# Nine of ten up products in high and low f32r parts, raw weights loaded from ScalarE's queue, and new written orders for five engines

## What is computed

```python
# state space: DI = 256 channels, DS = 16 states, 256 positions, per batch b
state = state * exp(delta_t * A) + (delta_t * u_t) * B_t
y_t   = sum_n state[:, n] * C_t[n]
x = x + tanh(g_xattn) * ((y + D * u) * silu(layernorm(x)))
# experts: xf = layernorm(x); 2 shared units and 8 experts, FF = 176
h_e   = silu(xf @ wg_e.T) * (xf @ wu_e.T)
x = x + tanh(g_ffn) * (sum_shared h_e @ wd_e.T + sum_e weight_e * (h_e @ wd_e.T))
```

## Time and profile before

| | us |
|---|---|
| median of 3 runs | 282.44 |
| lowest, highest | 282.11, 283.94 |
| the profiled execution, its own time | 282.1 |
| its span, first to last instruction | 280.3 |
| busy: VectorE / TensorE / GpSimd / ScalarE | 232.8 / 228.3 / 182.8 / 178.7 |

### The profile page before, as it was taken

The page is one execution under the profiler, slowest core; times in us unless marked ns, Lnnn a source line. Parts: engine busy times, 40 slices in busy tenths (PEclk is TensorE's granted clock), DMA queues, the critical chain, the costliest instruction groups (busy, mean ns, idle before and its releaser), DMA issues.

```text
span 280.3 us, 4168 instructions
## 1 busy us (share of the span) xinstructions
PE 228.3 (81%) x1093; PEld 172.5 (62%) x1093; DVE 232.8 (83%) x590; ACT 178.7 (64%) x536; POOL 182.8 (65%) x187
## 2 busy tenths in 40 slices
PE   8823874386972869999968996899999989999994
PEld 3412652064741447878747784688778768778783
DVE  2569999999999999799999988997998899663431
ACT  3578999963785895659675896567665572251221
POOL 0029989999999999957677789857865483120000
PEclk9975797559896558999997997999999999999999
DMA  6699970000024000000007000000000000000000
GB/s 177 210 314 384 306 299 0 0 0 2 0 118 187 0 1 0 19 4 0 19 6 299 0 5 16 4 0 19 2 1 19 4 0 0 19 0 2 21 0 21
DMA packets 9560, 17.36 MB, mean 62 GB/s; under 512 B 824, under 2 KB 8800, under 8 KB 8928
## 3 DMA queue, kind: packets, MB, share of 16 engines
q1 hardware_dynamic: 9248, 16.94, 17.3%
q10 hardware_dynamic: 288, 0.16, 0.2%
HBM read 15.97 MB, written 1.11 MB: 61 GB/s over the span
## 4 chain that ended last, share of the span: by engine, by line
PE 41%; DVE 30%; POOL 14%; issue 8%; ACT 5%; DVEq 1%; POOLq 0%
PE psD L452 15%; PE psU L600 10%; DVE hs L897 6%; POOL dbu L1011 6%; DVE hs L903 5%; POOL acc L1035 5%; DVE prod L914 4%; DVE ag L985 4%; PE psM L584 4%; DVE hcat L812 3%; PE psU L610 2%; PE psU L612 2%; PE psU L611 2%; DVE xh L847 2%; PE psD L529 2%
## 5 line engine op out<-in xcount | busy, mean ns | idle before, releaser
L1011 POOL TENSOR_TENSOR dbu<-du,bb 128x512 f32<-128x512 f32 x64 | 81.9, 1293 | 31.9 <-DVE du L380 19.2
L643 ACT ACTIVATE psA<-delta,aneg 128x127 f32<-128x127 f32 (+1 forms) x256 | 79.1, 357 | 14.6 <-DVE hs L897 7.6
L1035 POOL TENSOR_TENSOR acc<-acc,prod 128x512 f32<-128x512 f32 x42 | 53.5, 1273 | 16.6 <-DVE prod L914 15.5
L600 PE MATMUL psU<-wup,hnT 128*128 128x352 f32 x160 | 59.9, 500 | 2.9 <-DVE hcat L808 1.0
L772 ACT ACTIVATE tg<-psU 128x176 f32<-128x176 f32 x80 | 24.9, 313 | 49.2 <-PE psU L600 31.4
L903 DVE TENSOR_TENSOR_SCAN hs<-psA,ends,dbu 128x128 f32<-128x128 f32 x128 | 50.9, 461 | 0.1
L452 PE MATMUL psD<-wdn,hT 128*128 128x256 f32 x224 | 50.2, 380 | 0.0
L452 PEld LDWEIGHTS psD<-wdn,hT 128*128 128x128 f32 x224 | 42.2, 190 | 6.2 <-issue 0.3
L914 DVE TENSOR_TENSOR prod<-hs,psC 128x512 f32<-128x512 f32 x64 | 43.2, 681 | 2.3 <-issue 1.4
L600 PEld LDWEIGHTS psU<-wup,hnT 128*128 128x128 f32 x160 | 30.0, 204 | 15.4 <-issue 2.9
L985 DVE SCALAR_TENSOR_TENSOR ag<-tg,psU 128x176 f32<-128x176 f32 x80 | 25.7, 327 | 15.5 <-ACT tg L772 15.4
(11 more groups left out here) (116 smaller groups left out, 327.2 us busy)
## 6 DMA issues: line engine op xcount, KB each, us to landing
bb<-brows SPq DMA_DIRECT2D x3, 2048.0 KB, 7.1
hcat<-in_w_up SPq DMA_DIRECT2D x2, 880.0 KB, 8.9
wup<-in_w_up SPq DMA_DIRECT2D x2, 880.0 KB, 11.4
wdn<-in_w_down SPq DMA_DIRECT2D x1, 1664.0 KB, 14.1
x_sb<-in_x SPq DMA_DIRECT2D x4, 256.0 KB, 6.8
bb<-brows SPq DMA_DIRECT2D x1, 1024.0 KB, 4.7
out<-outb SPq DMA_DIRECT2D x8, 128.0 KB, 1.7
sel<-in_sel SPq DMA_DIRECT2D x1, 768.0 KB, 6.0
```

The source lines that it names most:

```text
L600: last = pe.matmul(dst, hnT[:, b % 2, k, lh * P:(lh + 1) * P], wup[:, j // 2, k, :], start=(k == 0), stop=(k == KT - 1))
L643: last = act.activation(dst[:, j, h, c:], delta[:, b % 2, h, l0 + c:l1], ACT.Exp, scale=aneg[:, h * DS + s0 + j:h * DS + s0 + j + 1])
L1011: pool.tensor_tensor(tile(dbu[:, m % DBU_RING]), du[:, b % 2, :, l0:l1].unsqueeze(1).broadcast_to(shape), bb[:, b % 2, s0:s0 + NS, l0:l1]. ...
L1035: pool.tensor_tensor(acc[:, p % 2], before, prod[:, i % PROD_RING], ALU.add).then_inc(s_add, 1)
```

## The change

1. In each tile only unit j = 0 remains a plain f32 product; units 1 to 9 use f32r parts. So nine high and nine low parts of the weights are made in place of five.
2. The raw weights of units 1 to 5 and of unit 0 are loaded by DMAs issued from ScalarE's queue at the very start, ahead of all its work. Those of units 6 to 9 are loaded into the same staging memory by a new SyncE task, `weights_more:0`, once five low parts are made; it stands between `dt:0` and `xproj:1`.
3. `up:j` of the first tile waits for its own part only, and `mul:0` no longer waits for the parts.
4. All lists are written anew. The scratch memory for dynamic DMA is set to 4096 bytes.

```diff
-NSPLIT = NU // 2
+NSPLIT = NU - 1
+WSTAGE = 5
...
-        wup = sb("wup", [P, NU - NSPLIT, KT, 2 * FF])
+        wup = sb("wup", [P, KT, 2 * FF])
...
-                        for k in range(KT):
-                            sp.dma_start(staged[:, :, k], w_up[:, 1::2, k]).then_inc(d_wst, 16)
-                        for k in range(KT):
-                            sp.dma_start(wup[:, :, k], w_up[:, 0::2, k]).then_inc(d_wup, 16)
...
+                elif task == "weights_more":
+                    sp.wait_ge(s_wlo, WSTAGE)
+                    sp.dma_start(staged[:, 0:NSPLIT - WSTAGE], w_up[:, 1 + WSTAGE:NU]).then_inc(d_wst[1], 16)
...
-                            if j % 2 == 0:
+                            if j == 0:
...
-                                if unit == 1:
-                                    pe.wait_ge(s_wlo, NSPLIT)
+                                if unit < NU:
+                                    pe.wait_ge(s_wlo, j)
...
-                                    w_hi, w_lo = whi[:, j // 2, k, :], wlo[:, j // 2, k, :]
+                                    w_hi, w_lo = whi[:, j - 1, k, :], wlo[:, j - 1, k, :]
...
             act.dma_start(par[:, :], params).then_inc(d_par, 16)
+            act.dma_start(staged[:, :], w_up[:, 1:1 + WSTAGE]).then_inc(d_wst[0], 16)
+            act.dma_start(wup[:, :, :], w_up[:, 0]).then_inc(d_wup, 16)
...
-                    if i == 0:
-                        act.wait_ge(d_wst, 16 * KT)
-                    act.copy(whi[:, i], staged[:, i]).then_inc(s_whi, 1)
+                    if i % WSTAGE == 0:
+                        act.wait_ge(d_wst[i // WSTAGE], 16)
+                    act.copy(whi[:, i], staged[:, i % WSTAGE]).then_inc(s_whi, 1)
...
-                if unit == 0:
-                    dve.wait_ge(s_wlo, NSPLIT)
```

More of the change, by code:

```diff
@@ L112 @@
[L112 to L116, removed]
@@ L167 @@
-        scan:61 gate:61 prod:61 scan:62 prod:62 scan:63 mul:60 mul:61 finish:5 prod:63 gate:62 mul:62 gate:63
-        mul:63 gate_y:7 residual:7 gate:64 mul:64 stats:7 gate:65 mul:65 variance:7 gate:66 mul:66 gate:67
-        mul:67 gate:68 mul:68 gate:69 mul:69 route:7 gate:70 mul:70 gate:71 mul:71 finish:6 gate:72 mul:72
-        gate:73 mul:73 gate:74 mul:74 gate:75 mul:75 gate:76 mul:76 gate:77 mul:77 gate:78 mul:78 gate:79 mul:79
-        finish:7
+        load:0 tap0:0 tap1:0 tap2:0 silu_u:0 split0:0 z_stats:0 split1:0 split2:0 z_stats:1 log_1:0 log_2:0
@@ new lines @@
+        delta0:0 delta1:0 delta2:0 tap0:1 z_stats:2 scan:0 prod:0 scan:1 scan:2 prod:1 scan:3 tap1:1 prod:2
+        tap2:1 prod:3 scan:4 scan:5 prod:4 prod:5 z_stats:3 silu_u:1 scan:6 scan:7 prod:6 prod:7 z_gate:0 scan:8
+        scan:9 split0:1 gate_y:0 split1:1 split2:1 residual:0 prod:8 prod:9 stats:0 variance:0 scan:10 scan:11
+        prod:10 prod:11 log_1:1 scan:12 prod:12 log_2:1 scan:13 route:0 tap0:2 tap1:2 scan:14 prod:13 prod:14
+        scan:15 scan:16 gate:0 gate:1 mul:0 prod:15 prod:16 tap2:2 scan:17 prod:17 scan:18 mul:1 prod:18 gate:2
@@ new lines @@
+        silu_u:2 mul:2 gate:3 gate_y:1 mul:3 residual:1 gate:4 mul:4 scan:19 scan:20 prod:19 prod:20 stats:1
+        gate:5 gate:6 split0:2 variance:1 z_gate:1 split1:2 mul:5 split2:2 scan:21 prod:21 scan:22 mul:6 scan:23
+        prod:22 prod:23 scan:24 scan:25 gate:7 gate:8 route:1 mul:7 mul:8 prod:24 prod:25 log_1:2 scan:26
+        scan:27 gate:9 log_2:2 gate_y:2 prod:26 prod:27 mul:9 residual:2 scan:28 scan:29 stats:2 variance:2
+        prod:28 prod:29 gate:10 gate:11 mul:10 mul:11 scan:30 scan:31 prod:30 finish:0 prod:31 gate:12 mul:12
@@ new lines @@
+        gate:13 mul:13 scan:32 scan:33 gate:14 gate:15 prod:32 prod:33 route:2 mul:14 mul:15 tap0:3 tap1:3
+        gate_y:3 tap2:3 scan:34 silu_u:3 residual:3 z_gate:2 stats:3 gate:16 variance:3 prod:34 mul:16 scan:35
+        scan:36 gate:17 gate:18 mul:17 mul:18 split0:3 prod:35 prod:36 split1:3 scan:37 scan:38 split2:3 gate:19
+        prod:37 mul:19 prod:38 route:3 scan:39 scan:40 prod:39 prod:40 gate:20 log_1:3 gate:21 mul:20 mul:21
+        scan:41 scan:42 finish:1 log_2:3 prod:41 prod:42 gate:22 gate:23 mul:22 mul:23 scan:43 scan:44 gate:24
@@ L191 @@
+        prod:57 prod:58 scan:61 scan:62 prod:59 features_lo:6 prod:60 prod:61 prod:62 prod:63 variance:7
+        features_lo:7
     """,
```

176 lines of the change are left out of this document (85 added, 91 removed).

## The result

The changed kernel takes 285.37 us (median of 20 runs, 283.71 to 286.5), the kernel before on the same chip 283.51 us (20 runs, 282.11 to 285.19). The ratio is 1.0068, with a 95% interval of 1.0051 to 1.0084: slower by 0.7%, 1.9 us. By the 1% that the prediction took as its bound this is no change. The forecast was 278.6 us, faster by 1.4%, with a range of 273 to 285 us; the time lies 0.4 us above the range, and on the other side of the kernel before. The profiled execution has a span of 284.1 us, 3.8 us longer than before.

The account below looks back on a forecast made before the run. Bounds: VectorE and GpSimd to 110 us, VectorE and TensorE to 240, then TensorE. Terms -0.9, -3.3, -1.3, +1.0, +0.7 sum to -3.8 us from 282.1, giving 278.3; median forecast 278.6 us, range 273 to 285.

Parts of the forecast that it names:

- TensorE, four more units: Expert units: each f32 unit made f32r saves 0.23 us, 4.4 us from 110 to 240 us and 1.8 us behind.
- VectorE, another order: VectorE's list: parting dependent neighbours saves 0.12 us each, 3.7 us: 0.9 before 110 us and 2.8 behind.
- 110 to 240 us, 3.3 us gained: Middle stage: VectorE's 2.8 us and TensorE's 4.4 us together gain 3.3 us, bounds 0 and 8.
- The end, 1.3 us: Behind the last scan: TensorE's cheaper units gain 1.3 us, bounds 0.5 and 1.8.
- Casts, 1.0 us: ScalarE and GpSimd, before 110 us: four more high and low parts cost 1.0 us, bounds 0 and 4.2.
- The start, 0.7 us: Before the first scan: early load delays it 2.6 us, early z_stats return 1.9; net +0.7 us, bounds -1.9 and +4.6.
- rival (c): Start: staged weights land late, delaying xproj_out behind ScalarE's cast; +4.6 instead of +0.7 us, 282.5 us; chance 0.1.
- the forecast's own wait: Start: z_stats:1 waits for all of x, landing about 17 us, so log_1:0 and the first scan come 2.6 us later.
- (b): Up to 240 us: gain hidden, down blocks and GpSimd set the pace as before; 282.8 us, chance 0.15.
- (d): TensorE, 110 to 240 us: idling more, its clock falls for 16 us, losing 8 us; 286.6 us, chance 0.12.
- (a): Whole kernel: VectorE's and TensorE's savings add up and x comes in time; -10.6 us, some 272 us, chance 0.12.

Follow-up runs that it names:

- 5: Kernel before, old lists, with units 2, 4, 6, 8 also f32r using odd units' parts, no added casts: 279.67 us, ratio 0.9893.
- 6: Run 1 with five f32r units instead of nine and without the four added pairs of casts: 288.09 us, ratio 1.0158 to the kernel before.
- 2: Changed kernel with unit 1's casts moved behind the first steps, early load kept: 289.06 us, ratio 1.0204 to the kernel before.
- 7: Run 1 with twelve scan/prod and gate/mul places in VectorE's list made dependent neighbours again: 285.35 us, ratio 1.0070 to the kernel before.
- 10: Run 9 with five scan/prod and six gate/mul places of VectorE's list paired, parting dependent neighbours: 285.52 us, ratio 1.0078 to the kernel before.
- 14: Run 9 with only the five scan/prod places paired: 283.65 us, ratio 1.0008 to the kernel before.
- 15: Run 9 with only the six gate/mul places paired: 283.86 us, ratio 1.0029 to the kernel before.
- 9: Old lists, nine f32r units, only units 1 to 3 loaded early, casts spread, z_stats early: 281.91 us, ratio 0.9967 to the kernel before.
- 1: Changed kernel with raw weights loaded late by SP as before and unit 1's casts behind the first steps: 283.69 us, ratio 1.0020 to the kernel before.
- 11: Run 1 without the f32r product of high features by low weights: 275.89 us, ratio 0.9748 to the kernel before.
- 12: Run 5 without the f32r product of high features by low weights: 275.79 us, ratio 0.9745 to the kernel before.
- 4: Old lists, nine f32r units, four added pairs of casts between steps 10 and 18, loads late: 286.78 us, ratio 1.0131 to the kernel before.
- 16: Changed kernel with z_stats:0 and 1 moved back behind delta2:0, load and cast still early: 288.12 us, ratio 1.0172 to the kernel before.
- 3: Kernel before with only its five staged units loaded from ScalarE's queue at the start: 283.41 us, ratio 1.0008.

## Why the prediction was wrong

**TensorE, four more units: right in kind, too large.** The f32r step of 0.16 us holds for nine units in a row. TensorE's timeline of the changed kernel:

```profile
243.31 0.40 PE L612 MATMUL psU<-whi,hnhi 128*128 128x352 f32 x1
243.55 0.32 PE L613 MATMUL psU<-wlo,hnhi 128*128 128x352 f32 x1
...
244.35 0.32 PE L612 MATMUL psU<-whi,hnhi 128*128 128x352 f32 x1
```

The first step of a unit behind other work is 0.24 us, the others 0.16, so from 243.31 to 244.35 us a unit takes 1.04 us; behind another f32r unit it takes 0.96. An f32 unit of the kernel before, by itself, takes 1.19 us (from 266.57 us to the next instruction at 267.76). The saving is 0.15 to 0.23 us, not 0.23 throughout: the prediction took both units of the pair in the earlier trace rows at 12 even steps, and the pair takes 1.04 + 0.96 = 2.00 us, not 1.92. With the old lists the products gave 3.0 us (5), where the terms had 4.4 and 1.8.

**VectorE, another order: this step failed.** The prediction priced the new lists by neighbours alone, 0.12 us for each that is parted, and by that they were a gain of 3.7 us. The runs show none: in the form of 6 the lists are a loss of 4.5 us, and with unit 1's pair of casts at its early place still about 0.6 us of loss, an estimate (6 less the price from 2) whose sign lies within the noise. The price itself has something to it, since bringing 24 dependent neighbours together cost 1.7 us (7), where 24 x 0.12 would be 2.9. But it isn't a price of the list: in the old lists parting them cost time (10, 14, 15). Of the Trainium skill's VectorE: DVE Perf Modes, "The DRAIN you can't avoid", the forecast weighed that the term is nothing, and left out that the same section lets a next operation that isn't held start earlier. For the single instruction the rows stood against the term being nothing. For the sum it came nearer than I did, but by luck: 1.7 us of the price are real (7), and something else outweighed them.

What I left out is where the new lists put everything else, the units above all. On TensorE's list, before, unit 9 stands behind spread_c:21, unit 19 behind spread_c:33, unit 49 behind spread_c:55. After, it is 27, 37 and 58. I had both lists and counted neighbours in them, but not this. The loss begins before 110 us. In experiment 6, with no late start and no added cast, neither VectorE nor GpSimd is full from 20 to 110 us, where they were busy 88.03 and 85.75 us before (columns as in the earlier trace rows):

```profile
20.00:110.00 90.00, 55.02 (x205) 38.25 (x206) 82.30 (x184) 69.00 (x201) 78.34 (x72) 0.68 0.30 108
```

So VectorE's list no longer paces this stage by itself. By step 32 this run is 3.7 us late, by the last scan 6.2 us, so a part is lost behind it too. TensorE's idle time is plainest from 110 to 140 us, in the kernel before and in the changed kernel:

```profile
110.00:140.00 30.00, 29.83 (x160) 24.70 (x160) 27.82 (x69) 20.23 (x66) 22.96 (x23) 1.00 0.03 10
```

```profile
110.00:140.00 30.00, 24.06 (x130) 20.16 (x128) 28.18 (x73) 19.38 (x67) 24.18 (x29) 0.93 0.02 6
```

TensorE idles 5.9 us of 30 with the new lists, at a clock of 0.93, and 0.2 us with the old ones; in experiment 9, with the old lists too, it is busy 29.64 us at the full clock. VectorE is about as busy in all three. Experiment 1, which has no late start, has 25.58 us here at a clock of 0.83, and experiment 6, with the old number of f32r units too, 24.40 at 0.94, so the idle time comes from the lists and neither from the late start nor from the products. TensorE's two longest waits in this window, which the kernel before doesn't have there and 6 has again, are for two of VectorE's tasks that still read a shared PSUM tile: the router weights (psD) and the silu of the convolution (psM). TensorE takes its list in order, so no later unit runs meanwhile:

```profile
PE psD L544 <- DVE wtok L980: 2.1, 1, 2.1
PE psM L586 <- DVE u L858: 1.1, 1, 1.1
```

Less than half of it is won back from 140 to 180 us, where TensorE idles 4.2 us instead of 6.7; the rest of these units come later, when TensorE is full. Unit 19's gate ends at 127.3 us before and 143.8 after, and tile 1's output is done at 137.2 us before and 157.5 after. That TensorE has the larger part in the end with the new lists is shown by 11 and 12. How much the later place of tiles 0 and 1 costs is not shown: no run moved these units alone, and the place of unit 1's pair of casts (2) accounts for most of the 4.5 us of 6.

**110 to 240 us, 3.3 us gained: failed with it.** By the last scan the changed kernel is 5.5 us behind (243.5 against 238.0), where the prediction expected it some 3.5 us ahead. Experiment 5 has the products without the new order, and its last scan is 1.1 us earlier than before.

**The end, 1.3 us: right.** From the last scan to the last output it is 40.1 us before (238.0 to 278.1) and 38.5 after (243.5 to 282.0), 1.6 us less.

**Casts, 1.0 us: right for spread ones only.** Between 5 and 9 lie 0.7%, some 2 us, for the added casts and the early load together, where the sum had 1.0 + 0.7. In GpSimd's full stretch the same four pairs cost 2.4%, 6.7 us (4 against 5), above the upper bound of 4.2 us; about a third of that is the wait for the second load. The duration of a low part was right, 1.682 us in the changed kernel. Its place was priced too low: the prediction took the early pair at the 1.7 us of the low part, and it is worth 3.8 us (2 against the changed kernel).

**The start, 0.7 us: this step failed too, in its parts; their sum came out near by luck.** Both waits of the prediction are there. The staged weights were issued at 1.6 us and landed at 14.6 us, 13.0 us later. The page's DMA issues (KB, median us from issue to landing):

```profile
hcat<-in_w_up ACTq DMA_DIRECT2D x1, 1760.0 KB, 13.0
```

That is rival (c), and by itself it puts du at 23.7 us (16). The copy to xdbl ran at 15.31 us instead of 11.27, 4.0 us late; du ended 5.1 us late. But the forecast's own wait was the longer one. All of x was there only at 19.4 us, not at 17, so dy started at 20.4 us and not near 18, and by itself that wait puts du at 25.0 us (2). The Trainium skill's DMA: Bandwidth & Descriptors, "Queues, rings and completion order", as the prediction read it, would have had these weights pass in one turn and land early; the trace shows 13.0 us, so its turns didn't help here. The reading counted 128 rows over 16 engines, 8 to an engine; in the first 16 us ScalarE's queue moved 576 packets, 36 to an engine, so the reading may be at fault and not the rule. The first scan came only 2.6 us later, since the two z_stats, 1.9 us, and two taps of batch 1, 1.5 us, no longer stand between du and it, and a third z_stats, 0.9 us, does. The taps are only put off. The term had +2.6 us for the wait; the load alone costs 5.2 us (2 against 1), its whole delay. What the delay takes in gives most of this back: 3.8 us for unit 1's pair of casts and 2.9 us for the two z_stats (16), each measured with the other in place, where the prediction had 1.7 and 1.9. So the changed kernel is only 1.4 us slower than 1.

**Rivals.** (b), the gain hidden, 282.8 us, named no loss by the order and fell short by 2.6 us; no rival had the lists themselves as the slower part. (d), 286.6 us, came nearest in time, but its condition, a clock below 0.93 between 110 and 240 us, didn't hold: it was 0.92 to 180 us and 1.00 behind, 0.96 over the whole (0.92 x 70 + 60, over 130) against 0.97 before. The difference is worth at most 2.1 us of full speed (126.5 - 124.4). It is not nothing: of the 20 runs of the changed kernel the six with the lowest mean clock, 0.856 to 0.874, took 286.1 us on average, the eight with the highest, 0.885 to 0.897, 284.5. Whether the lower clock makes a run longer or comes from longer pauses of TensorE, no run tells. (a) fell with the neighbours. By ratios the change is: lists in the form of 6 +1.6%, nine products with their casts in them -1.4%, early load +1.8%, unit 1's pair of casts into the time before du -1.4%, together +0.7% with rounding. The sum must come out, since each run stands on the one before; in another order the parts could have other sizes.

## What to carry to other kernels

When a written order changes, list for each engine where every task of the second phase stands against the steps of the first, and look for windows in which the engine that is alone at the end would idle earlier, as TensorE does here at 110 us. A price per neighbour on one engine holds only where that engine paces the stage and nobody waits for the later one of the pair. Price a moved task by what stands behind it and not by its length: one pair of casts, whose longer part takes 1.7 us, was worth 3.8 us by its place. Extra work for a full engine is best put into the idle time before its first task, and the rest spread; the four further casts cost 2.4% in one place, a late load included, and, with an early load, 0.7% in another, and the old order with nine units and spread casts was 0.3% faster than the kernel before. A load that is moved to the start costs nothing while nobody early waits for what it pushes back (3), and its whole delay where somebody does (2).

## What the runs showed of the hardware that I had not expected

- A large load from ScalarE's queue held SP's own loads back: x on SP's queue landed 13.4 us after its issue instead of 6.8 (medians of four), the 768 KB of sel 12.0 us instead of 6.0. The 1760 KB themselves took 13.0 us; at the 344 GB/s of the earlier trace rows they alone would take 5.2 us, an estimate.

- The first f32r product behind another kind of work takes one step of 0.24 us instead of 0.16, and behind an f32 unit 0.43 us (from 260.50 to 260.93 us in the kernel before).
